# A log-polar pooling convolution with batch norm: three sums along w moved from vector instructions to adding DMA transfers

## The reference, cut to what matters

```python
y = conv(x.reshape(B * C, 1, H, W), masks, pad=4)            # 12 bin averages for each channel
out = conv(y, w_conv1, stride=(4, 3)) + conv(x, w_center)    # mixes 12 x 256 channels, and the centre
out = out + b_center
mean, var = out.mean((0, 2, 3)), out.var((0, 2, 3))
out = (out - mean) * rsqrt(var + 1e-5) * gamma + beta
return relu(out + x)
```

## Time and profile before

| | |
|---|---|
| time of 3 runs | 1686.37 us median (1686.28 to 1686.71) |
| profiled execution | 1686.6 us |
| its span, first to last instruction | 1684.8 us |
| busy in the span | PE 1489.2 us, DVE 1531.3 us, ACT 645.3 us, POOL 2.7 us |
| one image in the steady part | 46.7 us |
| DMA over the span | 129.54 MB, mean 77 GB/s |

### The profile page before, as it was taken

The page is one execution under the profiler, slowest core; times in us unless marked ns, Lnnn a source line. Parts: engine busy times, 40 slices in busy tenths (PEclk is TensorE's granted clock), DMA queues, the critical chain, the costliest instruction groups (busy, mean ns, idle before and its releaser), DMA issues.

```text
span 1684.8 us, 21919 instructions
## 1 busy us (share of the span) xinstructions
PE 1489.2 (88%) x8468; PEld 1476.5 (88%) x8468; DVE 1531.3 (91%) x1455; ACT 645.3 (38%) x689; POOL 2.7 (0%) x21
## 2 busy tenths in 40 slices
PE   6899999999999999999999999999999999993000
PEld 6899999999999999999999999999999999993000
DVE  8999999999999999999999999999999999995423
ACT  3234343343333434334333343433433334434423
POOL 0000000000000000000000000000000000000000
PEclk8999999999999999999999999999999999997555
DMA  2010111001111011100111101111011110149999
GB/s 110 20 38 29 38 38 38 21 27 38 38 38 38 29 38 38 38 29 19 38 38 38 38 29 38 38 38 37 11 38 38 38 38 29 38 159 421 425 424 382
DMA packets 28615, 129.54 MB, mean 77 GB/s; under 512 B 3520, under 2 KB 3520, under 8 KB 28608
## 3 DMA queue, kind: packets, MB, share of 16 engines
q1 hardware_dynamic: 23744, 103.77, 17.0%
q10 hardware_dynamic: 4864, 25.69, 3.7%
HBM read 78.88 MB, written 50.58 MB: 77 GB/s over the span
## 4 chain that ended last, share of the span: by engine, by line
PE 50%; DVE 27%; issue 11%; SPq 5%; ACT 4%; DMA 3%; DVEq 0%; ACTq 0%
PE acc L625 17%; PE acc L627 16%; PE acc L626 16%; DVE pooled_split L403 6%; DVE pooled L402 6%; DVE inner_split L403 5%; SPq L266 3%; ACT inner_split L324 3%; DVE box L402 2%; DVE y_stage L402 2%; DVE row L402 2%; DMA phase<-x 2%; SPq L263 2%; DMA out<-phase 1%; ACT phase L394 0%
## 5 line engine op out<-in xcount | busy, mean ns | idle before, releaser
L334 ACT ACTIVATE pooled_split<-pooled 128x1456 fp32r<-128x1456 f32 x192 | 273.4, 1425 | 608.0 <-DVE pooled L402 608.0
L403 DVE TENSOR_TENSOR pooled_split<-pooled,pooled_split 128x1456 fp32r<-128x1456 f32 x192 | 317.4, 1667 | 0.3 <-ACT pooled_split L334 0.3
L625 PE MATMUL acc<-inner_split,w_first 128*128 128x406 f32 (+1 forms) x640 | 225.7, 353 | 36.3 <-DVE y_stage L402 25.0
L625 PE MATMUL acc<-pooled_split,w_first 128*128 128x364 f32 x768 | 253.6, 330 | 2.4 <-DVE pooled_split L403 2.4
L625 PE MATMUL acc<-pooled_split,w_outer 128*128 128x364 f32 x768 | 252.3, 329 | 1.1 <-DVE pooled_split L403 1.1
L626 PE MATMUL acc<-pooled_split,w_first 128*128 128x364 f32 x768 | 252.6, 329 | 0.0
L627 PE MATMUL acc<-pooled_split,w_first 128*128 128x364 f32 x768 | 252.5, 329 | 0.0
L626 PE MATMUL acc<-pooled_split,w_outer 128*128 128x364 f32 x768 | 252.2, 328 | 0.0
L627 PE MATMUL acc<-pooled_split,w_outer 128*128 128x364 f32 x768 | 251.8, 328 | 0.0
L627 PE MATMUL acc<-inner_split,w_first 128*128 128x406 f32 (+1 forms) x640 | 222.8, 348 | 0.0
L625 PE MATMUL acc<-inner_split,w_inner 128*128 128x406 f32 (+1 forms) x640 | 221.2, 346 | 1.1 <-DVE inner_split L403 1.1
(11 more groups left out here) (82 smaller groups left out, 2200.7 us busy)
## 6 DMA issues: line engine op xcount, KB each, us to landing
x_pad<-x SPq DMA_DIRECT2D x64, 392.0 KB, 3.3
y_dram<-y_stage SPq DMA_DIRECT2D x31, 784.0 KB, 5.0
phase<-y_dram SPq DMA_DIRECT2D x30, 784.0 KB, 28.3
phase<-x SPq DMA_DIRECT2D x30, 784.0 KB, 30.5
out<-phase ACTq DMA_DIRECT2D x30, 784.0 KB, 16.0
w_stage<-w_raw SPq DMA_DIRECT2D x2, 896.0 KB, 7.7
out<-x_pad ACTq DMA_DIRECT2D x2, 784.0 KB, 20.4
w_stage<-w_raw SPq DMA_DIRECT2D x2, 768.0 KB, 9.1
```

Of the source, the lines that this page charges most:

```text
L334: nc.scalar.activation(view(pooled_split, 2 * j * PAIR, (1, PAIR)), view(pooled, (PAIRS * c + j) % 2 * PAIR, (1, PAIR)), ACT.Copy)\
L403: sub = lambda out_, a, b: nc.vector.tensor_tensor(out_, a, b, ALU.subtract)
L625: nc.tensor.matmul(place, hi_w, hi_in, start=start, stop=False)
```

## The change

A second copy of x in DRAM, `x_wide`, has two zero columns on each side and four zero rows above and below each column, so a column takes TALL_PITCH = 36 numbers in place of 28. The buffers row2, row3 and ends get the same pitch. Each sum is now made by DMA: a plain transfer (SP) writes the first shifted copy of x into the buffer, and a transfer issued by POOL with `accum_op=ALU.add` adds the second; row3 takes two adding transfers one after the other. Their borders need no zeroing. The additions for row2, row3 and ends leave DVE, whose readers wait for the transfers instead. SP loads the next x as soon as v_ready is up.

```diff
+            def add_from(image, c, buf, first_column, n_columns):
+                return pool.dma_start(view(buf, 0, (1, n_columns * TALL_PITCH)),
+                                      x_wide[bass.ds(image, 1), :, c, bass.ds(
+                                          (first_column + EDGE) * TALL_PITCH, n_columns * TALL_PITCH)]
+                                      .rearrange("n p f -> p (n f)"), accum_op=ALU.add)
...
+            def image_sums(image):
+                for c in range(CH):
+                    s = CH * image + c
+                    wait_first(row3_begun, 16 * (s + 1))
+                    add_from(image, c, row3, -1, W + 2).then_inc(row3_second, 16)
+                    wait_first(row2_begun, 16 * (s + 1))
+                    add_from(image, c, row2, -1, W + 3).then_inc(row2_ready, 16)
+                    wait_first(row3_second, 16 * (s + 1))
+                    add_from(image, c, row3, 0, W + 2).then_inc(row3_ready, 16)
+                    wait_first(ends_begun, 16 * (s + 1))
+                    add_from(image, c, ends, 2, W).then_inc(ends_ready, 16)
...
         @block.sync
...
+            def begin_sums(image, c):
+
+                s = CH * image + c
+                wait_from_one(sp, box3_ready, s)
+                begin_sum(image, c, row3, W + 2, row3_begun)
+                wait_from_one(sp, pooled_ready, PAIRS * s - 1)
+                begin_sum(image, c, row2, W + 3, row2_begun)
+                wait_from_one(sp, pooled_ready, PAIRS * s)
+                begin_sum(image, c, ends, W, ends_begun)
...
             def image_steps(image, first=False, last=False):
-                if not last:
-                    for c in range(CH):
-                        sp.wait_ge(x_used, CH * image + c + 1)
+                for c in range(CH):
+                    if not last:
+                        sp.wait_ge(v_ready, CH * image + c + 1)
                         load_x(image + 1, c)
-                if not first:
-                    sp.wait_ge(y_ready, CH * image + FREE)
-                    sp.dma_start(y_dram[bass.ds(image - 1, 1)].rearrange("n p f -> p (n f)"),
-                                 y_stage[:, :]).then_inc(y_saved, 16)
+                    if c == 0:
+                        begin_sums(image, 1)
+                    elif not last:
+                        begin_sums(image + 1, 0)
+                    if c == 0 and not first:
+                        sp.wait_ge(y_ready, CH * image + FREE)
+                        sp.dma_start(y_dram[bass.ds(image - 1, 1)].rearrange("n p f -> p (n f)"),
+                                     y_stage[:, :]).then_inc(y_saved, 16)
...
             load_x(0, 0)
             load_weights(0)
+            begin_sums(0, 0)
             load_x(0, 1)
             load_weights(1)
```

On DVE:

```diff
-                    wait_from_one(dve, pooled_ready, PAIRS * s)
-                    add(view(row2, ROW2_H + 4, (ROW2_H, W + 1), (1, H)), columns(-1, 1, W + 1),
-                        columns(0, 1, W + 1)).then_inc(row2_ready, 1)
-
                     dve.wait_ge(inner_hi_ready, 2 * s + 1)
...
-                    dve.wait_ge(row2_ready, s + 1)
-                    add(view(row3, 1, (ROW3_H, W + 2), (1, H)), view(row2, 4, (ROW2_H, W + 2), (1, H)),
-                        columns(0, 1, W + 2)).then_inc(row3_ready, 1)
-                    add(view(ends, 2, (ENDS_H, W), (1, H)), columns(-2, 1, W), columns(2, 1, W))\
-                        .then_inc(ends_ready, 1)
-
-                    dve.wait_ge(row3_ready, s + 1)
-                    add(view(row3v, 2, (ROW3V_H, W + 2), (1, H + 1)), view(row3, 0, (ROW3_H, W + 2), (1, H + 1)),
-                        view(row3, 1, (ROW3_H, W + 2), (1, H + 1))).then_inc(row3v_ready, 1)
+                    dve.wait_ge(row3_ready, 16 * (s + 1))
+                    add(view(row3v, 2, (ROW3V_H, W + 2), (1, H + 1)),
+                        view(row3, RIM - 1, (ROW3_H, W + 2), (1, H + 1)),
+                        view(row3, RIM, (ROW3_H, W + 2), (1, H + 1))).then_inc(row3v_ready, 1)
...
                     dve.wait_ge(box4_ready, s + 1)
+                    dve.wait_ge(row2_ready, 16 * (s + 1))
...
+                    dve.wait_ge(ends_ready, 16 * (s + 1))
                     short_sum(s, c, 0)
```

More of the change, by code:

```diff
@@ L5, with conv_bn_relu_program @@
 from concourse import mybir
-def conv_bn_relu_program(nc, x, w_raw, b_center, gamma, beta, out, y_dram):
+def conv_bn_relu_program(nc, x, x_wide, w_raw, b_center, gamma, beta, out, y_dram):
     F32 = mybir.dt.float32
@@ L16, in conv_bn_relu_program @@
     IMAGES, P, CH, W, H = x.shape
+    EDGE, RIM = 2, 4
+    TALL_PITCH = H + 2 * RIM
     CHANNELS = P * CH
@@ L53, in conv_bn_relu_program @@
     PAIR = 4 * HALF_PLANE
-    ROW2_H, ROW3_H, ROW3V_H, BOX4_H, BOX3_H, ENDS_H = H + 8, H + 3, H + 5, H + 3, H + 4, H + 4
+    ROW3V_H, BOX4_H, BOX3_H = H + 5, H + 3, H + 4
+    ROW2_H = ROW3_H = ENDS_H = TALL_PITCH
     X_PAD = (W + 4) * H
@@ L174, in conv_bn_relu_program @@
         inner_lo_ready = sem("inner_lo_ready")
+        row2_begun = sem("row2_begun")
         row2_ready = sem("row2_ready")
+        row3_begun = sem("row3_begun")
+        row3_second = sem("row3_second")
         row3_ready = sem("row3_ready")
+        ends_begun = sem("ends_begun")
+        sum_turns = sem("sum_turns")
         row3v_ready = sem("row3v_ready")
@@ L214, in conv_bn_relu_program @@
         block = ctx.enter_context(nc.Block())
-        ZEROED = 17
+        ZEROED = 12
         @block.gpsimd
@@ L224, in _ @@
                          view(inner, 0, (MIDDLE, 2), (PITCH, U + 1)), view(inner, MIDDLE - 1, (MIDDLE, 2)),
-                         row2[:, :],
-                         view(row3, 0, (ROW3_H, W + 2)), view(row3, H + 1, (ROW3_H, W + 2), (1, 2)),
                          view(row3v, 0, (ROW3V_H, W + 2), (1, 2)), view(row3v, H + 3, (ROW3V_H, W + 2), (1, 2)),
-                         view(box3, 0, (BOX3_H, W + 2)), view(box3, H + 3, (BOX3_H, W + 2)),
-                         view(ends, 0, (ENDS_H, W), (1, 2)), view(ends, H + 2, (ENDS_H, W), (1, 2))):
+                         view(box3, 0, (BOX3_H, W + 2)), view(box3, H + 3, (BOX3_H, W + 2))):
                 if edge.dtype == F32R:
@@ L234, in _, with wait_first @@
             assert n == ZEROED
+            def add_from(image, c, buf, first_column, n_columns):
[3 more added lines that the diff above has]
+                                      .rearrange("n p f -> p (n f)"), accum_op=ALU.add)
+            def wait_first(semaphore, count):
+                pool.wait_ge(semaphore, count)
+                nc.gpsimd.sem_inc(sum_turns, 1)
+            def image_sums(image):
[9 more added lines that the diff above has]
+                    add_from(image, c, ends, 2, W).then_inc(ends_ready, 16)
+            image_sums(0)
+            with pool.Fori(1, IMAGES) as image:
+                image_sums(image)
         @block.sync
@@ L241, in load_x, with begin_sum @@
                     .then_inc(x_loaded[c], 16)
+            def begin_sum(image, c, buf, n_columns, begun):
+                sp.dma_start(view(buf, 0, (1, n_columns * TALL_PITCH)),
+                             x_wide[bass.ds(image, 1), :, c, 0:n_columns * TALL_PITCH]
+                             .rearrange("n p f -> p (n f)")).then_inc(begun, 16)
+            def begin_sums(image, c):
[6 more added lines that the diff above has]
+                begin_sum(image, c, ends, W, ends_begun)
             def load_weights(c):
@@ L495, in short_sum @@
                            view(box3, BOX3_H + 1 + 4 * m, (BOX3_H, 2), (2 * BOX3_H, u), (1, h)),
-                           view(ends, 6 * m, (ENDS_H, 2), (2 * ENDS_H, u), (1, h)))
+                           view(ends, RIM - 2 + 6 * m, (ENDS_H, 2), (2 * ENDS_H, u), (1, h)))
             def lo_of_pooled(s, c, j):
@@ L551, in image_steps @@
                             transform_weights(1)
-                    dve.wait_ge(ends_ready, s + 1)
-                    nc.vector.sem_inc(x_used, 1)
                     dve.wait_ge(row3v_ready, s + 1)
@@ L558, in image_steps @@
                     add(view(box3, 1, (BOX3_H, W + 2), (1, H + 2)), view(row3v, 1, (ROW3V_H, W + 2), (1, H + 2)),
-                        view(row3, 1, (ROW3_H, W + 2), (1, H + 2))).then_inc(box3_ready, 1)
+                        view(row3, RIM, (ROW3_H, W + 2), (1, H + 2))).then_inc(box3_ready, 1)
                     dve.wait_ge(box4_ready, s + 1)
+                    dve.wait_ge(row2_ready, 16 * (s + 1))
                     pooled_sums(s, c, 0, box4, 0, 4 * BOX4_H + 3, BOX4_H, row2, 0, 5 * ROW2_H + 8, ROW2_H)
@@ L699, in per_partition @@
         return np.ascontiguousarray(np.asarray(v).reshape(128, -1))
+    x_cols = np.ascontiguousarray(
+        np.asarray(x).reshape(images, 128, halves, height, width).transpose(0, 1, 2, 4, 3))
+    x_wide = np.pad(x_cols, ((0, 0), (0, 0), (0, 0), (2, 2), (4, 4))).reshape(images, 128, halves, -1)
     arrays = {
-        "x": np.ascontiguousarray(
```

(3 more changed lines are left out.)

1 line of the change is left out of this document (removed).

## The result

The changed kernel takes 1734.77 us (median of 4 runs, 1729.66 to 1740.71) against 1686.36 us, a ratio of 1.029 (95% interval 1.025 to 1.032): slower by 48 us, where 28 us less were forecast. The profiled execution took 1735.86 us, its span 1734.2.

A forecast was written before the change was run, and what follows sets the result against it. A ring of PE, ACT and DVE through take_y was taken as the bound, with PE's own pace 45.94 us per image as floor; 1686.6 - 23.4 (steady part) - 5 (start) = 1658 us, range 1650 to 1672.

The forecast's parts named there:

- What bounds the kernel, and what can be gained: Ring of PE, ACT and DVE through take_y costs PE 0.78 us per image; 23.4 us over 30 steady images.
- Removed from DVE: row2, row3 and ends, 2.99 us in each of 64 steps, 191 us busy; row2's part only lengthens the wait for ACT.
- The length of the series: Row3's three transfers in one buffer, box3 to row3v: 16.4 to 19.0 us, taken as 17.5, with 19.0 free.
- rival A: Row3's series is late and sets the pace, image twice (series + 3.99) us; slower, up to 1857 us; chance 0.28.
- first addition: Row3's first adding transfer: 5.0 us by the tail's rate to 6.3 by the slope of plain transfers, bytes counted twice.
- second addition, row2's ahead of it: Row3's second adding transfer, 5.0 to 6.3 us, plus 1.5 for row2's addition ahead on POOL, sharing the engines.
- handing over: POOL's own work to issue each of row3's two additions: 0.5 us each, with no row to show it.
- sign of a broken forecast: Adding transfers taking over 6.5 us from issue to landing would break the forecast.
- The margin: Row3's series of 17.5 us just under 19.0 free; ends 11.7 (additions quick as plain transfers) and 22.1 (slow as slowest load).
- Doubled bytes: An addition reads buffer and x_wide, so its bytes count twice: 1080 KB for 540 KB.
- DMA engines full (B): Additions hold the DMA engines for three passes at 303 GB/s, image 59.5 us; slower, about 2080 us; chance 0.14.
- Start: Image 1, where PE waits 8.6 us: 5 us gained, ends 0 and 11, with first sums waiting behind x and weights.

The follow-up runs named there:

- take_y early: Kernel before, no DMA sums: take_y moved ahead of the two short sums and a lo part in DVE's order; 1659.12 us, ratio 0.984.
- row3's additions first and take_y early: Changed kernel with POOL issuing both row3 additions before row2's, and take_y moved ahead of DVE's short sums; 1661.84 us, ratio 0.986.
- row3 first: Changed kernel with POOL issuing both additions of row3 before that of row2, same transfers otherwise; 1668.97 us, ratio 0.990.
- changed kernel with take_y early: Changed kernel, additions in its own order, with take_y moved ahead of the short sums; 1730.92 us, ratio 1.024.
- the series alone: Changed kernel without the additions of row2 and ends, row3's two kept; 1665.06 us, ratio 0.987.
- copies in place of additions: Changed kernel with POOL's four transfers per step overwriting instead of adding, same bytes from DRAM, issues and waits; 1660.13 us, ratio 0.985.

## Why the prediction was wrong, point by point

*What bounds the kernel, and what can be gained: right.* PE's own pace of 45.9 us per image, 0.78 us away, was reached by each run in which nobody waited for a series: e.g. 900.00 of 900 us busy with take_y early. The 23.4 us of the steady part were real.

*Removed from DVE: right.* Its busy time fell by 170 us (the 191 were a sum of durations, and neighbours on DVE overlap by some 0.09 us, which makes 17 us for 192 instructions), and its wait for ACT doubled, from 42.2 to 83.1 us, as said of row2.

*The length of the series: the step that failed.* The mechanism was named (rival A), but the sum that was to keep it away was too small. Its terms, with the means over steps 3 to 63 of the changed kernel, from issue to landing:

| term | forecast | measured |
|---|---|---|
| plain copy | 3.9 | 3.6 |
| first addition | 5.55, out of 5.0 to 6.3 | 6.25 |
| second addition, row2's ahead of it | 5.55 + 1.5 | 8.6 |
| handing over | 1.0 | 1.6 |
| sum, where 19.0 were free | 17.5 | 20.07 |

The term that was mis-sized is the price of the additions: 14.8 us for the two instead of 12.6. 1.4 to 1.6 of these 2.2 us belong to the bare price. Of its two estimates the prediction's 6.3, by the slope of the earlier trace rows, was right, and the 5.0, by the tail's rate, was not. The other 0.6 to 0.8 are row2's addition, put at 1.5 and measured at 2.1 to 2.3. The prediction's own sign of a broken forecast, additions of over 6.5 us, came with medians of 7.2 and 8.8. Handing over adds 0.6: 0.2 before SP's issue, 0.7 before each of POOL's. The store of y was named as lying in the way and given no price; the second addition takes 1.6 us more before steps c = 1, where that store is issued. Where take_y and the store came earlier (row3's additions first and take_y early) the same difference was 0.3, against 1.3 with row3 first alone; in the changed kernel with take_y early it was 1.2, against 1.6. That fits the store as the cause and does not prove it.

Row2's addition was not most of the error, but it decided the sign: with it behind, the series lands after 18.1 us, under the 19.0, and the time is 1669. The forecast without its 1.5 us would have been 16.0, so the other terms together were 2 us short even there.

*The margin.* 17.5 against 19.0, with ends of 11.7 and 22.1, was thin, and the text itself said that 2 us more decide. The sum was 2.6 us off.

*Doubled bytes: right.* An addition holds the engines 1.85 times as long as a copy (1.93 times in the run with row3 first, 48.1% of 1666.7 us). The Trainium skill, "Collectives: The Full Stack", section on the bandwidth ceiling, has two source reads and half the rate for the add of a ReduceScatter, and the measured factor is near that. POOL's issues were not held up by DVE: they took 0.864 us in the mean of 192, with 0.86 us for those at 523.21, 526.25 and 530.36, all of them begun while DVE ran an instruction with two inputs in SBUF. The 3.7 us that rival A added for such a hold-up did not appear. It rested on the Trainium skill, "SBUF — State Buffer", section "Who interferes with whom", whose rule is about GpSimd's reads of SBUF; the same section reports that such instructions did not stall DMAs in a probe, and the trace agrees.

*DMA engines full (B): did not happen.* The share was 0.82 in a steady image (0.71 to 0.98 follow from the prediction's 16.4 and 22.5 us of 22.97), and 0.86 in the faster kernel with row3's additions first.

*Start: wrong sign.* 5 us gained were forecast, 9 lost (7.4 by step 3). The first copy landed at 9.8 us, as forecast. The two first additions were put at 5 to 6 us each and took 10.1 and 7.1. The row for that, a load of 768 KB in 9.1 us beside others, was on the table and used only for the upper end.

*Rival A in numbers.* For its bound of 22.1 us it gave 1857. At the measured 20.07 the same formula gives 48.1 us per image, 1.4 more; 31 of these and the 9 of the start give 1739, against 1735.9 for the profiled execution. The formula was right.

## What to carry to other kernels

When work moves from an engine to DMA, count the transfers that must follow one another in one buffer, with the hand-over between them (here 0.7 us), and set that sum against the time for which the buffer is free; the share of the DMA engines says little about it. On a queue with both urgent and patient transfers, the urgent ones go first, since a patient one ahead costs both its own traffic and the wait for its inputs: two lines swapped were worth 66 us here. And look first whether the wait to be removed can be had by order alone: moving one block of DVE's program brought 27 us with no transfer at all.

## What the runs showed of the hardware

An adding transfer of 540 KB takes 6.2 us from issue to landing (the series alone) with only plain ones beside it. A copy issued from POOL takes 4.9 (copies in place of additions), one from SP 3.6. The bytes of an addition hold the DMA engines 1.85 times as long as a copy's (changed kernel against copies). POOL needs 0.86 us to issue one, 0.53 for a copy (the same two). From the landing of one to POOL's issue of the next that waits for it, 0.7 us pass. With another addition issued 4 us ahead of it, row3's second takes 8.6 us in the mean; with that one issued right behind it 6.5, and 6.2 with none. Not expected was how much one suffers beside a stream of plain loads: 10.1 us for the first addition of the changed kernel, and 9.9 to 10.5 in the seven other runs that have it, among them the one without additions of row2 and ends. A copy in its place took 7.8. Why is open.
